# Edge stage of a graph network: feature columns turned by transposing transfers in place of TensorE products and ScalarE copies

## What is computed

```python
i_idx, j_idx = edge_index[0], edge_index[1]
msg_input = concatenate([node[i_idx], node[j_idx], edge_features], axis=-1)   # 256 + 256 + 16
h = relu(msg_input @ mW1 + mb1)                                               # 512 per edge
messages = h @ mW2 + mb2
aggregated = segment_sum(messages, i_idx, num_segments=3125)
...
```

## Time and profile before

| | |
|---|---|
| three runs | 2049.65, 2052.21, 2060.61 us; median 2052.21 |
| the profiled execution's own time | 2049.62 us |
| its span, first to last instruction | 2047.8 us |
| PE, DVE, POOL, ACT busy | 89%, 75%, 62%, 39% of the span |
| edge stage | 549 to about 1217 us |

### The profile page before, as it was taken

One profiled execution on the slowest core, in us unless ns is written; L12 is line 12 of the kernel. 1 busy time (PEld: TensorE's weight loads), 2 busy tenths in 40 slices (PEclk: granted clock), 3 DMA queues, 4 the chain that ended last, 5 costly groups with the idle time before them and its releaser, 6 DMA issues. The chain is left out here.

```text
span 2047.8 us, 34486 instructions
## 1 busy us (share of the span) xinstructions
PE 1817.7 (89%) x8786; PEld 1237.3 (60%) x8786; DVE 1542.7 (75%) x4650; ACT 797.9 (39%) x1975; POOL 1262.3 (62%) x1463
## 2 busy tenths in 40 slices
PE   4577887777399999999999998989979999999999
PEld 2344544444255555555555556666657888788887
DVE  7887787777489999999999988988988345445333
ACT  0122222222155665665665656656664112113000
POOL 2777777777788888888888859999979000000000
PEclk7677777888699999999999999999999999999999
DMA  5111111111276766666766785222236344343333
GB/s 163 39 58 51 52 58 58 58 58 56 69 197 195 198 195 195 198 195 195 196 196 194 194 173 163 69 66 68 72 92 185 93 124 124 93 126 121 109 108 110
DMA packets 181705, 254.12 MB, mean 124 GB/s; under 512 B 29244, under 2 KB 144761, under 8 KB 181514
## 3 DMA queue, kind: packets, MB, share of 16 engines
q0 software_dynamic: 47888, 126.25, 22.6%
q1 hardware_dynamic: 104696, 102.31, 16.4%
q10 hardware_dynamic: 28930, 23.35, 3.5%
HBM read 202.35 MB, written 49.37 MB: 123 GB/s over the span
## 5 line engine op out<-in xcount | busy, mean ns | idle before, releaser
L1009 POOL DMA_INDIRECT brow<-B_rows,rows x440 | 467.8, 1063 | 114.9 <-issue 58.4
L380 POOL DMA_INDIRECT src_list<-ring,ring_row x392 | 385.8, 984 | 156.7 <-issue 117.6
L1959 PE MATMUL pO<-F,y 128*128 128x512 f32 x1728 | 431.5, 404 | 4.7 <-DVE y L1770 3.2
L1959 PEld LDWEIGHTS pO<-F,y 128*128 128x128 f32 x1728 | 326.7, 190 | 79.8 <-DVE y L1770 4.0
L1332 POOL TENSOR_SCALAR src_oh<-iota,src_s 128x128 bf16<-128x128 bf16 x426 | 285.1, 685 | 39.9 <-PE pC L1475 21.8
L1059 PE MATMUL pNode<-hid_whole,oh 128*128 128x512 f32 x440 | 228.7, 601 | 4.9 <-DVE sums L1195 4.5
L1125 ACT ACTIVATE turned<-pC 128x256 fp32r<-128x256 bf16 x220 | 84.7, 385 | 279.9 <-PE pC L1038 279.9
L1348 DVE TENSOR_SCALAR dst_oh<-iota_cw,dst_s 128x458 bf16<-128x458 f16 x568 | 181.7, 366 | 0.0
L1061 PE MATMUL pNode<-hid_upper,oh 128*128 128x512 f32 x220 | 175.3, 797 | 0.0
L1475 PE MATMUL pC<-dst_oh,src_oh 128*128 128x458 bf16 x568 | 157.4, 361 | 16.6 <-SPq L1430 8.3
L824 PE MATMUL pP<-U,upto 128*128 128x182 bf16 x385 | 49.6, 280 | 136.4 <-DVE posf L587 136.4
(11 more groups left out here) (306 smaller groups left out, 3413.1 us busy)
## 6 DMA issues: line engine op xcount, KB each, us to landing
raw<-C_rows SPq DMA_DIRECT2D x54, 768.0 KB, 4.4
C_rows<-c_rows ACTq DMA_DIRECT2D x175, 114.5 KB, 1.7
raw_first<-C_rows SPq DMA_DIRECT2D x18, 768.0 KB, 4.4
rows<-src_list SPq DMA_DIRECT2D x110, 100.0 KB, 2.8
brow<-B_rows,rows POOLq DMA_INDIRECT x440, 3.8
U_parts<-part_u SPq DMA_DIRECT2D x25, 256.0 KB, 2.0
B_rows<-bst SPq DMA_DIRECT2D x25, 256.0 KB, 2.1
src_list<-ring,ring_row POOLq DMA_INDIRECT x392, 2.2
```

The costliest lines, as they stand in the source:

```text
L380: nc.gpsimd.indirect_dma_start(dr.src_list[:, :, :].rearrange("p t w -> (p t) w"), bass.IndirectOffsetOnAxis(ap=ring_row[:, k % RING, t:t ...
L1009: nc.gpsimd.indirect_dma_start(brow[:, t % BR, :], None, dr.B, bass.IndirectOffsetOnAxis(ap=rows_i[:, m % LCS, j, 1:2], axis=0)).then_inc( ...
L1959: last = mm(pO[m % 2][half][:, :], y[:, win, part, half * P:(half + 1) * P], F[:, n % FS, :], start=(win == 0 and part == 0), stop=False)
```

## The change

The two feature turns of `turn`, and the ACT copy behind them, are taken out. SP instead issues one transposing transfer for each tile: it reads 128 rows of 256 bytes from the sorted list in HBM (the 96 feature numbers and, behind them, 32 numbers of the next tile's row in the list) and leaves them as columns in `turned_e`, now a ring of six tiles, three pairs, in SBUF. A transfer into a slot waits for the end of `edge` of the pair that used it (`edge_done`). The two transfers of a pair share one semaphore (`e_in`), on which `edge` waits as well. The product on line 1048 reads the first 96 partitions. The load of `ub2` and the quads' loads stand in SP's queue between the transfers. The gathers of a pair now share one semaphore too (`b_in`).

```diff
-        turned_e = g.sb("turned_e", [EW, 2, 2 * P], BF16)
+        TE = 6
+        turned_e = g.sb("turned_e", [P, TE, P], BF16)
+        feat_rows = dr.src_list[:, :, :].rearrange("p t w -> p (t w)").bitcast(BF16)
...
-        b_in = [g.sem(f"b_in{n}") for n in range(BR)]
+        e_in = [g.sem(f"e_in{n}") for n in range(TE // 2)]
+        b_in = [g.sem(f"b_in{n}") for n in range(BR // 2)]
...
-            for m in range(QUADS):
+            def load_rows(m):
                 if m >= LCS:
                     sp.wait_ge(pre_ready, 2 * (m - LCS + 1))
                     sp.wait_ge(cols_copied, m - LCS + 1)
                 sp.dma_start(rows[:, m % LCS, :, :], dr.src_list[:, m * LC:(m + 1) * LC, :]
                              ).then_inc(rows_in[m % LCS], 16)
-                if m == LCS:
-                    sp.dma_start(ub2[:, :], io["L0_gnn_ub2"].partition_broadcast(P)).then_inc(ub_in, 16)
+
+            def turn_features(t):
+                if t >= TE:
+                    sp.wait_ge(edge_done, (t - TE) // 2 + 1)
+                sp.dma_start_transpose(turned_e[:, t % TE, :], feat_rows[:, 2 * ROW * t + 4:2 * ROW * t + 4 + P]
+                                       ).then_inc(e_in[t // 2 % (TE // 2)], 16)
+
+            for m in range(LCS):
+                load_rows(m)
+            sp.dma_start(ub2[:, :], io["L0_gnn_ub2"].partition_broadcast(P)).then_inc(ub_in, 16)
+            for t in range(NT):
+                turn_features(t)
+                m = t // LC + LCS - 1
+                if t % LC == LC - 1 and LCS <= m < QUADS:
+                    load_rows(m)
...
-                for n in range(2):
-                    last = nc.tensor.transpose(pT[p % 2][0:EW, (2 + n) * P:(3 + n) * P],
-                                               rows16[:, q % LCS, j + n, 4:4 + EW], keep.ident16[:, :])
...
+                pe.wait_ge(e_in[p % (TE // 2)], 32 * (p // (TE // 2) + 1))
...
-                    mm(to, turned_e[:, p % 2, n * P:(n + 1) * P], keep.we[:, :], start=True, stop=False)
+                    mm(to, turned_e[0:EW, (2 * p + n) % TE, :], keep.we[:, :], start=True, stop=False)
...
                     nc.scalar.activation(turned[:, i % 2, :], pT[i % 2][:, 0:2 * P], ACT.Copy,
-                                         accum_out=keep.pair_deg[:, i:i + 1])
-                    nc.scalar.copy(turned_e[:, i % 2, :], pT[i % 2][0:EW, 2 * P:4 * P]).then_inc(turn_copied, 1)
+                                         accum_out=keep.pair_deg[:, i:i + 1]).then_inc(turn_copied, 1)
...
-                for t in (2 * p, 2 * p + 1):
-                    dve.wait_ge(b_in[t % BR], 16 * (t // BR + 1))
+                dve.wait_ge(b_in[p % (BR // 2)], 32 * (p // (BR // 2) + 1))
```

More of the change, by code:

```diff
@@ L1010, in _ @@
                     brow[:, t % BR, :], None, dr.B,
-                    bass.IndirectOffsetOnAxis(ap=rows_i[:, m % LCS, j, 1:2], axis=0)).then_inc(b_in[t % BR], 16)
+                    bass.IndirectOffsetOnAxis(ap=rows_i[:, m % LCS, j, 1:2], axis=0)).then_inc(b_in[t // 2 % (BR // 2)], 16)
                 w, k = divmod(t - 4 * LC - 1, 4 * LC)
@@ L1034, in turn @@
                 for n in range(2):
-                    nc.tensor.transpose(pT[p % 2][:, n * P:(n + 1) * P], oh_upper[:, q % OHQ, j + n, :, 1],
+                    last = nc.tensor.transpose(pT[p % 2][:, n * P:(n + 1) * P], oh_upper[:, q % OHQ, j + n, :, 1],
                                         keep.ident16[:, :])
-                for n in range(2):
-                    last = nc.tensor.transpose(pT[p % 2][0:EW, (2 + n) * P:(3 + n) * P],
-                                               rows16[:, q % LCS, j + n, 4:4 + EW], keep.ident16[:, :])
                 last.then_inc(turn_done, 1)
```

## The result

The kernel with the change takes 2096.0 us (2090.93 to 2097.21, 3 runs) against 2052.21: ratio 1.0194, 95% interval 1.0165 to 1.0223. It is slower by 44 us where 24 us less were forecast. The range held it (2006 to 2220), the likeliest case and its sign did not. The profiled execution of after has a span of 2094.2 us.

A forecast was written before the change was run, and what follows sets the result against it. PE was taken as the bound, DVE and POOL about 0.2 us a pair behind. Only PE's 24 us counted, the added costs being hidden: 2049.6 - 24 = 2025.4 us (2028 on the median), range 2006 to 2220.

The forecast's parts named there:

- the likeliest case: Whole kernel: faster, 24 us less, with its own range 2008 to 2042 us and chance 0.51.
- PE's gain: Edge stage on PE: dropping two products saves 0.11 us a pair start to start, 24 us over 220 pairs.
- rival 4: PE's freed time lost to a gap before line 1048 or DVE's register loads: 0 to 10 us gained, chance 0.12.
- The transfer's cost on the DMA engines: Edge stage, 16 DMA engines: 0.12 us of all 16 a transfer, bounds 0.09 and 0.72, costed at nothing.
- The 11 ns a row of the forecast's bounds: One engine's time per row in the sort's scatter, used for the bounds 0.09 and 0.72 us a transfer.
- Rival 1: The 16 DMA engines fill in the edge stage: up to +111 us, 2163 us, chance 0.17.
- rival 3: Transfers do not overlap, each starting when the one before has landed: +313, 2365 us, chance 0.09.
- The failed step: PE's new wait for both transfers ahead of the feature product: free, with 1.9 us margin in each quad's first pair.
- The first term: SP's issue of one transposing transfer: taken as 0.33 us, like a quad's plain load.
- The second term: Transfer's landing after issue: 3.3 us, between load and gather, bounds 2.0 and 8.9.
- The rival that came true: Transfers land late for PE in each quad's first pair: with L = 6.5, +45, 2097 us, chance 0.11.
- its formula: Late-landing pair time T = (6.23 + L) / 4, L being the second transfer's issue to landing; slower from L = 5.7.

The follow-up runs named there:

- after: The kernel with the change as described, measured and traced against the kernel before it: 2096.0 us against 2052.21, ratio 1.0194.
- l_half_unread: Changed kernel with 220 narrow transposing transfers, every second tile only, nobody waiting, product reading a tile of ones: ratio 0.995 to the kernel before.
- k_wide_unread: Changed kernel with one transposing transfer of 128 x 512 B a pair, nobody waiting, product reading a tile of ones: 2045.14 us, kernel before 2053.96.
- f_wide_2: Changed kernel with one waited transposing transfer of 128 x 512 B a pair instead of two of 128 x 256 B: ratio 1.0159 to the kernel before.
- m_wide_te12: Changed kernel with one waited transposing transfer of 128 x 512 B a pair and a feature ring of 12 tiles: 2076.83 us, kernel before 2053.96.
- n_quad: Changed kernel with one waited transposing transfer of 128 x 1024 B per four tiles and a feature ring of 12; its time is not in the text.

## Why the prediction was wrong

- **PE's gain: right for three pairs in four, too large in all.** It is 0.11 us from start to start, and a step of PE lasts 2.84 us. But in `l_half_unread`, where no wait for a transfer is left, only three of four steps last 2.83 to 2.85 us in the median (2.94 to 2.95 before). Every fourth, the one behind each reload of the address in A, lasts 2.99, as before (2.99). Of 24 us, 8.8 to 10.4 are measured with 220 unread transfers, nothing on the slower chips. That is what rival 4 said of the register loads, with 0 to 10 us gained; which engine's loads they are, and whether the 220 transfers take a share, is not shown.
- **The transfer's cost on the DMA engines: right enough.** The packets add to 2.59 us of one engine a transfer, 0.16 us of all 16, against 0.12, as 128 packets of 256 bytes, 20 ns each. The 11 ns a row of the forecast's bounds were no price of a small piece: by the earlier trace rows that queue's packets had 800 bytes in the mean, 5.88 MB in 7327. The share rose to 0.84 (0.80 forecast) while PE waited. Rival 1 is out, and rival 3 with it: a next transfer is issued 1.24 us after the last, which lands in 4.
- **The failed step: "So the wait costs nothing, by a margin of 1.9 us".** Two terms under it were mis-sized, and it took both: the issue used 1.2 us of the margin and the landing 1.3.
- **The first term: "The sum goes by 0.33" for the issue.** It measured 1.23 us in the median of the 440. The second transfer's issue moved from 1.93 to 3.12 us after E(p-3): 0.8 of these 1.2 us are the first transfer's hold, 0.3 the addition, which ends at 1.58 and not 1.27, and 0.1 the gap behind the load. The hold also leaves SP next to no slack, 5.5 of every 5.7 us. The row of a plain load was the nearest one, but not of the same kind of instruction, and I named no upper end from rows. The Trainium skill's ratio (DMA: Bandwidth & Descriptors, the table beside fast DGE) gave an estimated 0.40 us; the trace does not agree, with 3.75 times the plain load's 0.328. The Trainium skill's 1309 ns for a transfer (VectorE: DVE Perf Modes, The three transpose paths) is near the 1.23 us that the queue is held, though not the 4 to 4.5 us after which the features may be read. Read as a time between transfers, as rival 3 did, it should have been put into SP's queue: 4 x 1.31 + 0.33 is an estimated 5.6 of the 5.7 us, and the trace agrees with that reading.
- **The second term: "I take 3.3" for the landing.** It measured 4.56 us in the tight pairs, since the last increment comes 1.2 us after the data in the median and 2 to 3.5 in the long waits. With loads it was 0.34 us, so the rows I took it from could not show that.
- **The rival that came true** is the second, with its place (first pair of a quad), its engine (PE ahead of the feature product) and nearly its time: 2097 forecast with L = 6.5, 2096.0 measured. The way to it was another: its formula has the issue at 1.93. With 3.12 and 4.56, T = (3.12 + 4.56 + 1.45 + 2.85) / 4 = 3.00 us; the measured mean of 3.17 has the long tail in it, since early landings give nothing back. So the 2097 were met by luck, with an issue too early and an L too long. Its chance of 0.11 rested on a margin of 1.9 us made of two durations that no row had shown.
- **The balance.** From first to last addition it is 637.4 us in `l_half_unread` and 640.5 in `k_wide_unread`, on another chip of the same speed, and 694.8 in the change. Of the 54 to 57 us between, 50.1 are PE's waits for the last increment and an estimated 3 to 4 the half clock. The rest is not traced.
- **Not foreseen at all:** a second price, which needs no wait. It shows on the slower chips, 3.3 to 3.7% for 440 unread transposing transfers in three measurements. On a chip like the first 220 unread ones show none; all 440 unread were not measured there.

## What to carry to other kernels

Price an instruction that the trace does not show from both sides also where it only occupies a queue, and then count that queue over one period of its ring: here five issues fill 5.5 of 5.7 us. A transfer's landing is the last increment of its semaphore, not its last byte, and a deeper ring lengthens a lead only if nothing else in the same queue waits for something later. On TensorE such a turn costs 0.055 us in a stream; a transposing transfer of this size has to be issued some 6 us ahead, by a queue with 1.2 us to spare, before the 0.11 us of a pair can be earned. Here even that came in three pairs of four.

## What the runs showed of the hardware

- A transposing transfer holds its issuing queue 1.23 us for 128 x 256 B (median, `after`), 1.17 to 1.24 for 128 x 512 B (`f_wide_2`, `m_wide_te12`) and 1.20 for 128 x 1024 B (`n_quad`); a plain one of the same 128 x 256 B 0.42 (median), a quad's load 0.33.
- Its completion is signalled 1.22 us (median; 1.96 at nine in ten) after its last data packet, and beside such transfers the plain loads' completion slips from 0.34 to 0.73 (`after`) and 1.21 us (`k_wide_unread`).
- On chips where the kernel before takes 2201 to 2226 us, transposing transfers bring pauses of 2.3 to 2.6 us in the mean on VectorE (30 to 42 with 440 transfers unread or with long rings, 24 in the change itself, 10 with plain ones, 9 to 12 with none, 3 in the kernel before). In the pause that was read closely the gathered data lay ready and PE's signals came 2.3, 1.0 and 1.0 us late. That this has the same cause as the late increments is a guess; no run separates them.
- PE's granted clock was 0.50 from 716.1 to 719.5 us in `after`, behind 1.79 us in which PE stood idle; two products took 1.91 us there and 1.03 at 705.62.
